# A two-layer attention and expert kernel: two dense batches instead of three, 28 routed pairs instead of 26, and gates by tanh in pieces

## The reference, cut to what matters

```python
x = L0_attn_x                                    # 16 batches x 256 tokens x 128, float32
# layer 0
xn = layernorm(x)
s = attention0(xn)                               # 16 heads of 8, relative bias
f = moe0(xn)                                     # 8 experts of 128x512x128, top 2 + a shared branch, layer norm
x = x + s * silu(f)
# layer 1
xn = layernorm(x)
s = attention1(xn)                               # 8 heads, attention over channels
# moe1: router 128 -> 256 (gelu) -> 4 logits, softmax, top 2 of 4 experts
out = 0
for e in range(4):
    h = gelu((xn * token_mask[e]) @ We1[e] + be1[e])     # 128 -> 512
    out = out + (h @ We2[e] + be2[e]) * combine_w[e]     # 512 -> 128
x = x + s * silu(out)
```

## Time and profile before

| | us |
|---|---|
| median of 3 runs | 760.46 |
| lowest and highest of them | 759.81 and 763.92 |
| the profiled execution's own time | 761.59 |
| its span, from the first to the last instruction | 759.8 |

### The profile page before, as it was taken

One profiled execution on the slowest core, in us unless ns is written; L12 is line 12 of the kernel. 1 busy time (PEld: TensorE's weight loads), 2 busy tenths in 40 slices (PEclk: granted clock), 3 DMA queues, 4 the chain that ended last, 5 costly groups with the idle time before them and its releaser, 6 DMA issues. The chain is left out here.

```text
span 759.8 us, 17184 instructions
## 1 busy us (share of the span) xinstructions
PE 680.9 (90%) x5393; PEld 475.5 (63%) x5393; DVE 543.9 (72%) x1277; ACT 477.1 (63%) x926; POOL 435.5 (57%) x393
## 2 busy tenths in 40 slices
PE   3887888999999999999999999799999898999890
PEld 2751333333333333379999888798888687989780
DVE  6889999999999999943333477664659893643356
ACT  4774677788888888864444648569652464544451
POOL 6912456899999999945555445400007767544452
PEclk9997999999999999999999999999999999999996
DMA  7975542223323233277888877450001523888865
GB/s 237 314 204 170 174 123 68 76 76 93 99 84 91 77 102 87 76 211 234 260 282 261 280 234 229 127 143 0 3 1 47 178 72 103 235 245 242 267 207 173
DMA packets 96462, 117.46 MB, mean 155 GB/s; under 512 B 10552, under 2 KB 72296, under 8 KB 96408
## 3 DMA queue, kind: packets, MB, share of 16 engines
q1 hardware_dynamic: 88376, 100.22, 45.0%
q0 software_dynamic: 8032, 16.58, 6.3%
HBM read 82.30 MB, written 34.32 MB: 153 GB/s over the span
## 5 line engine op out<-in xcount | busy, mean ns | idle before, releaser
L1473 ACT ACTIVATE work<-wide,work 128x256 f32<-128x256 f32 (+1 forms) x324 | 131.1, 469 | 133.5 <-PE wide L1057 132.4
L811 POOL DMA_INDIRECT yg_dram<-work x135 | 133.3, 987 | 135.7 <-DVE work L2071 108.8
L1634 DVE TENSOR_REDUCE work<-wide 128x4 bf16<-128x1024 f32 x128 | 154.4, 1224 | 8.2 <-PE wide L919 7.6
L1068 PE MATMUL wide<-work 128*128 128x128 f32 x1272 | 155.0, 275 | 0.4 <-ACT work L1473 0.4
L1068 PEld LDWEIGHTS wide<-work 128*128 128x128 f32 x1272 | 148.9, 192 | 1.6 <-ACT work L1473 0.8
L1057 PE MATMUL wide<-xT,work 128*128 128x256 f32 (+1 forms) x552 | 129.3, 377 | 7.4 <-issue 5.4
L1057 PEld LDWEIGHTS wide<-xT,work 128*128 128x128 f32 x552 | 98.1, 190 | 20.1 <-issue 8.0
L772 POOL TENSOR_TENSOR work<-work,biasT 128x1024 f32<-128x1024 f32 x30 | 71.1, 2372 | 39.9 <-ACT work L1402 39.3
L772 POOL TENSOR_TENSOR yy<-yy,biasT 128x1024 f32<-128x1024 f32 x30 | 71.2, 2372 | 17.4 <-ACT yy L1402 16.7
L919 PE MATMUL wide<-biasA,turnb 128*128 128x512 bf16 x256 | 80.0, 395 | 0.0
L1411 ACT ACTIVATE yy<-yy 128x1024 f32<-128x1024 f32 x64 | 67.4, 1055 | 18.8 <-DVE yy L1944 17.9
(11 more groups left out here) (311 smaller groups left out, 1157.2 us busy)
## 6 DMA issues: line engine op xcount, KB each, us to landing
work<-in_wcat SPq DMA_DIRECT2D x73, 578.0 KB, 4.6
xg_dram<-empty SPq DMA_DIRECT2D x35, 260.0 KB, 2.8
work<-xg_dram SPq DMA_DIRECT2D x66, 130.0 KB
stk_dram<-yy SPq DMA_DIRECT2D x16, 384.0 KB, 3.2
work<-stk_dram SPq DMA_DIRECT2D x64, 96.0 KB
work<-stk_dram SPq DMA_DIRECT2D x64, 64.0 KB
yy<-yg_dram SPq DMA_DIRECT2D x8, 512.0 KB, 6.6
biasT<-ext_dram SPq DMA_DIRECT2D x8, 384.0 KB
```

The costliest lines, as they stand in the source:

```text
L811: g.indirect_dma_start(out=yg_dram[l], out_offset=bass.IndirectOffsetOnAxis(ap=yid[v][:, s_:s_ + 1].bitcast(u32), axis=0), in_=yb[v][:, s_ ...
L1068: last = mm(YP[u][:, s_ * D:(s_ + 1) * D], hb[u][:, c, s_ * P:(s_ + 1) * P], wb[v][:, HID + c * D:HID + (c + 1) * D], start=(c == 0), stop ...
L1473: A(hb[u][:, c, 0:n * P], bank[2 + 2 * u + c // 2][:, (c % 2) * TS:(c % 2) * TS + n * P], ACT.Gelu, bias=wb[v][:, bc:bc + 1]).then_inc(m[" ...
L1634: V.tensor_reduce(nmax[:, :, 2 * place(t):2 * place(t) + 2].rearrange("p c e -> p e c"), into[:, :].rearrange("p (e c k) -> p e c k", e=2, ...
```

## The change

- `ND = 2`: 8 dense passes instead of 12. `NDA` becomes 6 between the layers, and two still come behind the router. `PAIRS` becomes 28, so there are 31 routed tiles.
- The same eight router turns are spread over six passes (`TURNED`), two turns in passes 2 and 4.
- Fetches of the first layer's tiles 16 to 31 come in three chunks instead of two, all ahead of the fourth expert's weights.
- Between the layers DVE normalises tiles 16 to 23 itself (`normalise_third`), and ACT does the Silu of tiles 16 to 31 after all six passes, with the table loads placed by hand (`load_table`). The `keep_dense` calls are spread in another way.
- The gate of the second layer is written as 0.5 z s (1 + tanh(z / 2)): `gate_start` (DVE: 0.5 z s), `half_tanh` (ACT), `gate_scale` and `gate_add` (DVE). It is cut into five pieces, of tiles 0 to 3, 4 to 11, 12 to 18, 19 to 24 and 25 to 31. The first two and the start of the third are placed among the routed tiles. Two of the six parts of the output are stored before the last wait for the stores.
- After the last routed tile DVE waits until POOL has issued its last store (`sent`) before it goes on with the gates.
- `route_pe` stands ahead of the last `down_rows` behind the router, and `keep_dense(NDA)` ahead of the counts.

```diff
-ND = 3
+ND = 2
-OUT_PARTS = ((0, 12), (12, 19), (19, 25), (25, 29), (29, T))
-CHUNKS = (((0, 8), (8, 16), (16, 24), (24, T)), ((0, 12), (12, 19), (19, 25), (25, T)))
-GATED = ((0,), (1,), (2,), (3, 4))
+OUT_PARTS = ((0, 4), (4, 12), (12, 19), (19, 25), (25, 29), (29, T))
+CHUNKS = (((0, 8), (8, 16), (16, 20), (20, 24), (24, T)), ((0, 12), (12, 19), (19, 25), (25, T)))
+GATES = ((0, 4), (4, 12), (12, 19), (19, 25), (25, T))
-TURN = {0: 0, 1: 1, 2: 2, 3: 3, 5: 4, 6: 5, 7: 6, 8: 7}
+TURNED = ((0,), (1,), (2, 3), (4,), (5, 6), (7,))
-NDJ = ND * E1
-NDA = NDJ - 2
+PASSES = tuple((b, e) for b in (0, 1) for e in range(E1))
+NDJ = len(PASSES)
+NDA = len(TURNED)
...
     # SP
+                    if l and j == NJC + 1:
+                        store_part(0)
...
                         if e == E1 - 1:
                             stored_through(nj)
-                            fetch(2, 0)
-                            fetch(2, 1)
+                            for q in range(2, 5):
+                                fetch(q, 0)
+                                fetch(q, 1)
                         sp.dma_start(wb[e], wcat1[e * P:(e + 1) * P, :]).then_inc(moe[1][f"W{e}"], 16)
-                    fetch(3, 0)
-                    fetch(3, 1)
                 else:
+                    store_part(1)
                     stored_through(nj)
...
     # POOL
             store_outputs(1, NJ1)
+            pool.sem_inc(com[1]["sent"], 1)
...
     # PE
             for j in range(NDA):
                 v = j % NWB
                 if j < NWB:
                     pe.wait_ge(m[f"W{v}"], 16)
-                pe.wait_ge(pre[1]["xT"], j // E1 + 3)
-                up_rows(m, j, v, xTd[j // E1])
+                pe.wait_ge(pre[1]["xT"], PASSES[j][0] + 3)
+                up_rows(m, j, v, xTd[PASSES[j][0]])
+                router_turn(TURNED[j][0])
                 if j == 1:
                     pe.wait_ge(moe[0]["y"], NJ0 + 4)
                 if j:
                     down_rows(m, j - 1, (j - 1) % NWB)
+                for b in TURNED[j][1:]:
+                    router_turn(b)
+            router_logits(NB // 2 - 1, 1)
             down_rows(m, NDA - 1, (NDA - 1) % NWB)
...
     # ACT, between the layers
             for j in range(NDA):
+                if j == 4:
+                    normalise_gate(3)
                 gelus(moe[1], j, j % NWB, 16)
+                for b in TURNED[j]:
                     hidden(b, b % 2)
...
-                if j in (4, 5):
-                    normalise_gate(j - 2)
-                elif j == 6:
-                    silu(0, 2)
-                    silu(0, 3)
+            load_table(ACT.Silu, 0)
+            silu(0, 2)
+            silu(0, 3)
+            load_table(ACT.Gelu, 1)
...
     # ACT, routed tiles
+                    if l and j == SPANS[-1][0] * NWB:
+                        half_tanh(0)
                     gelus(m, j + DENSE[l], j % NWB, j // NWB * 16 + (32 if l else 16))
+                    elif j == NJB + 7:
+                        half_tanh(1)
...
+            def half_tanh(i):
+                lo, hi = GATES[i]
+                act.wait_ge(com[1]["z"], i + 1)
+                A(yy[:, 1, lo:hi, :], yy[:, 0, lo:hi, :], ACT.Tanh, scale=0.5).then_inc(com[1]["silu"], 1)
...
     # DVE, routed tiles
+                    if l and j == NJC + 2:
+                        gate_scale(1)
+                    elif l and j == NJC + 3:
+                        gate_add(1)
                     outputs(j, j % NWB, j // NWB)
+                    elif j == NFULL + 5:
+                        gate_start(0)
+                    elif j == SPANS[-1][0] * NWB + 1:
+                        gate_scale(0)
+                    elif j == SPANS[-1][0] * NWB + 2:
+                        gate_add(0)
                     elif j in (NJB + 5, NJB + 7):
                         add_choices(1, (j - NJB - 5) // 2)
+                    elif j == NJB + 6:
+                        gate_start(1)
+                    elif j == NJC + 2:
+                        gate_start(2)
                     elif j == NJC + 3:
                         add_choices(1, 2)
...
     # DVE, between the layers
+            for q in (2, 3, 4):
+                lo, hi = CHUNKS[0][q]
+                add_choices(0, q)
+                add_shared(lo, hi)
+                gate_stats(lo, hi)
+                if q > 2:
+                    keep_dense(q - 3)
             finish_half(1, com[0]["stats"])
+            normalise_third()
             gamma_beta(2)
+            keep_dense(2)
+            gamma_beta(3)
+            keep_dense(3)
+            add_gated(2)
+            row_stats(16, 24)
+            add_gated(3)
+            row_stats(24, T)
+            finish_half(1, com[0]["x1"])
+            router_logits(0)
+            keep_dense(4)
+            keep_dense(5)
...
     # DVE, the end
             experts(1, NJ1)
-            for q in range(3):
-                gate_and_add(q)
-            add_choices(1, 3)
-            gate_and_add(3)
+            dve.wait_ge(com[1]["sent"], 1)
+            gate_scale(2)
+            gate_add(2)
+            gate_start(3)
+            gate_scale(3)
+            gate_add(3)
+            add_choices(1, 3)
+            last = len(GATES) - 1
+            gate_start(last)
+            for part in (last, last + 1):
+                gate_scale(last, part)
+                gate_add(part)
```

More of the change, by code:

```diff
@@ L43 @@
 STACK_ROUNDS = (5, 6, 10, 11, 12, 13, 14, 15)
-TURN = {0: 0, 1: 1, 2: 2, 3: 3, 5: 4, 6: 5, 7: 6, 8: 7}
+TURNED = ((0,), (1,), (2, 3), (4,), (5, 6), (7,))
 TD = ND * S // P
-NDJ = ND * E1
-NDA = NDJ - 2
+PASSES = tuple((b, e) for b in (0, 1) for e in range(E1))
+LATE = ()
+NDJ = len(PASSES)
+NDA = len(TURNED)
+LAST_PASS = [max(j for j in range(NDJ) if j % 4 == v) for v in range(4)]
+assert all(e == j % 4 for j, (_, e) in enumerate(PASSES))
 def tiles_for(experts, tokens):
@@ L668, in _ @@
                         fetch(3, k)
-            ov = out.rearrange("(t p) d -> p t d", p=P)
-            for i, (lo, hi) in enumerate(OUT_PARTS):
-                sp.wait_ge(com[1]["x1"], i + 1)
-                sp.dma_start(ov[:, lo:hi, :], yy[:, 0, lo:hi, :]).then_inc(s_out, 16)
+            for i in range(2, len(OUT_PARTS)):
+                store_part(i)
             sp.wait_ge(s_out, 16 * len(OUT_PARTS))
@@ L1164, in _, with router_turn @@
             pe.wait_ge(moe[0]["gelu"], NJ0 * 4 + 8)
-            for b in range(ND):
+            def router_turn(b):
+                pe.wait_ge(pre[1]["xT"], min(b + 2, NB // 2 - 1) + 3)
+                if b:
+                    router_logits(b - 1, (b - 1) % 2)
+                router_hidden(b, b % 2)
+                if b + 3 < NB // 2:
+                    transpose_normalised(b + 3)
+            for b in range(3):
                 transpose_normalised(b)
@@ L1191, in _ @@
             pe.wait_ge(pre[1]["lg"], 2 + 2)
-            for j in (NDA, NDA + 1):
-                up_rows(m, j, j % NWB, xTd[j // E1])
-            down_rows(m, NDA, NDA % NWB)
+            for j in range(NDA, NDJ):
+                up_rows(m, j, j % NWB, xTd[PASSES[j][0]])
+                if j > NDA:
+                    down_rows(m, j - 1, (j - 1) % NWB)
+            route_pe(1, E1, bank[0], bank[1])
+            down_rows(m, NDJ - 1, (NDJ - 1) % NWB)
             for k in range(2):
@@ L1569, in _ @@
             experts(1, NJ1)
-            for q in range(4):
-                silu(1, q)
+            for i in range(2, len(GATES)):
+                half_tanh(i)
         @block.vector
@@ L1606, in rsqrt, with take_stats @@
                 st.link(V.scalar_tensor_tensor(y, t1, RE, y, ALU.add, ALU.mult))
[L1608 to L1609 removed]
+            def take_stats(src, lo, hi):
+                for t in range(lo, hi):
                     st.did(V.bn_stats(stats[:, t, :], src(t)))
@@ L2130, in add_choices, with add_shared, gate_stats, row_stats @@
                     ins.then_inc(com[1]["z"], 1)
-            def add_shared(q):
-                z = yy[:, 0, q * 8:q * 8 + 8, :]
+            def add_shared(lo, hi):
+                z = yy[:, 0, lo:hi, :]
                 dve.wait_ge(pre[0]["shg"], 2)
-                st.link(V.scalar_tensor_tensor(z, sh_sb[:, q * 8:q * 8 + 8, :], 0.5, z, ALU.mult, ALU.add))
-            def gate_stats(q):
-                take_stats(lambda t: yy[:, 0, t, :], q)
-            def row_stats(q):
-                take_stats(lambda t: xres[:, t, :], q)
+                st.link(V.scalar_tensor_tensor(z, sh_sb[:, lo:hi, :], 0.5, z, ALU.mult, ALU.add))
+            def gate_stats(lo, hi):
+                take_stats(lambda t: yy[:, 0, t, :], lo, hi)
+            def row_stats(lo, hi):
+                take_stats(lambda t: xres[:, t, :], lo, hi)
+            def normalise_third():
+                dve.wait_ge(com[0]["stats"], 2)
+                for t in range(16, 24):
+                    z = yy[:, 0, t, :]
+                    st.did(V.tensor_scalar(z, z, mean[:, t:t + 1], rstd[:, t:t + 1], ALU.subtract, ALU.mult))
```

(10 more changed lines are left out.)

115 lines of the change are left out of this document (44 added, 71 removed).

## The result

The changed kernel takes 769.29 us in the median of 8 runs (766.04 to 770.98), the kernel before 761.11 (8 runs, 759.81 to 763.92): a ratio of 1.0095, 95% interval 1.0075 to 1.0115. A second series gave 1.0108 (1.0091 to 1.0125). The change is a loss of about 8 us. I had forecast a loss of 4.3 us, to 764.8, and a range of 761 to 768, so the sign was right and the size was not.

What follows compares the result with a forecast made beforehand. PE was taken to bound the routed tiles, DVE and PE together the stretch between the layers. Terms -4.0 + 2.0 - 0.2 + 7.5 - 0.4 + 0.5 - 1.1 = +4.3 us took the median from 760.46 to 764.8, range 761 to 768.

Steps and rivals of the forecast that it cites:

- Between the layers, -4.0: Four fewer dense passes between the layers free 14.1 us of PE, but the Silus and DVE's last stretch leave 4.0 gained.
- The rival by which PE's passes were the bound: Between the layers: PE's passes are the limit, so the whole 14.1 us is gained, giving 752.0 us; chance 0.1.
- The clock after the wait, +2.0: PE idles 11.3 us between the layers, so the router's work resumes at half clock: 2.0 us lost.
- Route and attention, -0.2: Behind the router: `keep_dense(NDA)` fits into DVE's wait for the counts, one fewer stands ahead of the attention: 0.2 us gained.
- Two more pairs, +7.5: Routed tiles: two more pairs at 3.73 us of PE each, hidden by nothing, cost 7.5 us.
- the waits among the tiles, -0.4 + 0.5: PE's idle times among routed tiles: the one behind `weigh_dense` shrinks by 0.4 us, SP's waits for stores add 0.5.
- The tail, -1.1: After the last matmul: last store issued 0.5 us sooner, last fetch 0.7 shorter, a DVE step 0.1 longer: 1.1 us gained.
- Tanh beside Gelu: ACT among the routed tiles: tanh and any table loads, at most 3.7 us, stay hidden: 0, at most +1 us.
- the rival on the other side: Between the layers: PE's passes bound, all 14.1 us gained, 752.0 us; said to decide from 5.8 us more gain; chance 0.1.

Runs made afterwards that it cites:

- silu_early: The changed kernel with the two Silus and their table loads put ahead of the Gelu of the sixth dense pass: ratio 1.0060 to the kernel before.
- clock_kept: The changed kernel with 48 matmuls on constants added where PE would idle between the layers: ratio 1.0061 to the kernel before.
- fetch_later: The kernel before with SP's wait for the stores, and the four fetches behind it, one tile later in the queue: ratio 0.9959, 758.62 us.
- two_empty_pairs: The kernel before with two more routed pairs that hold no token, and nothing else changed: ratio 1.0188.
- repaired: The changed kernel with silu_early's order, 16 matmuls on constants behind the sixth pass and the fetches one tile later: ratio 1.0000 to the kernel before, 760.93 us.
- gates_late: The changed kernel with two DVE gate steps moved behind the last outputs and the second piece's store behind the last fetches: ratio 1.0117 to the kernel before.
- store_late: The changed kernel with only the store of the second output piece moved behind the last fetches: ratio 1.0100 to the kernel before.
- gates_alone: The kernel before with only the tanh gates in pieces (also dropping one semaphore wait in the second layer's attention): ratio 1.0011.
- gates_alone2: The same as gates_alone, with the add of the first gate piece four tiles earlier: ratio 0.9995 to the kernel before.
- gates_and_fetch: The kernel before with the changes of gates_alone2 and fetch_later together: ratio 0.9985.

## Why the prediction was right in kind and too small

1. *Between the layers, -4.0.* Right: -3.6 in the first profile, -3.9 in the second. PE ended its passes 14 us sooner and waited, because the Silu came last on ACT and DVE's stretch came behind it. silu_early moved only ACT's order and moved the end by 3.3 us. The rival by which PE's passes were the bound is out.
2. *The clock after the wait, +2.0.* Right: 1.8 in the first profile, 2.3 in the second, and gone in clock_kept.
3. *Route and attention, -0.2.* **Failed.** It was +1.6 in the first profile (1.4 to the ranking, 0.2 in the attention) and +0.3 in the second. I let the clock fall once and come back for good. It fell again over the last two dense passes, for long in the first profile and for a shorter time in the second. Over all 14 profiles the length of these up products and the way to the ranking go together: without a fall 3.72 us, and the ranking after 7.2 us (five profiles, the kernel before among them); with a short fall mostly 5.41 us, and 7.3 to 7.6 us (six); with a long one 6.6 to 6.8 us, and 8.5 to 8.7 us (three). The three long ones are all of kernels with the whole pause of 11 us, of which there are four profiles. The short one also comes in fetch_later and two_empty_pairs, which have no pause, and in clock_kept, which fills it. So the pause does not cause this fall by itself; but it was there in all seven profiles with the changed stretch and in two of seven without. What sets it off is open.
4. *Two more pairs, +7.5, and the waits among the tiles, -0.4 + 0.5.* Right in mechanism: +6.6 in one profile, +8.3 in the other, +7.6 by the forecast; what the second profile has more is mostly idle time of PE, 4.9 us in the stretch against 3.5 (4.4 before). The 7.5 us more of busy time, the 3.74 us of a pair and two_empty_pairs confirm that nothing hides the pairs. The wait of 1.64 us stayed for the reason given: with the fetches one tile later it shrinks to 0.17 us in repaired.
5. *The tail, -1.1.* **Failed on the fetch**: +0.4 in the first profile, +0.3 in the second. The rows of the last store landed 0.5 us sooner, as written, and the last gate was 0.15 us longer. The 0.5 was partly luck: I had DVE keep still until the last store was issued. It doesn't, and the stores stay short because its gate steps happen to start just behind them (see gates_late). The fetch was 0.66 us longer instead of 0.7 shorter: less output beside it was to make it quicker. It took 5.25 to 5.59 us in all eight kernels with 28 pairs, two_empty_pairs with its old gates and old stores among them, and 4.61 to 4.82 in all six with 26. So it follows the number of pairs and neither the gates nor store_late's store. With 26 pairs the gates took only 0.1 to 0.2 us off it (4.66 in gates_alone, 4.73 in gates_alone2, against 4.82). The code makes `xg_dram` and `yg_dram` larger with it; whether their place in memory is the cause wasn't tried. The gates, which I gave this term to, do take 0.8 us from the tail with 26 pairs, and the whole kernel gains nothing by them (gates_alone2, gates_and_fetch).
6. *Tanh beside Gelu.* Right to cost it at nothing, and by less than I argued: I had hidden two table loads, and there are none. Timeline of ACT in the kernel after:
```profile
737.34 1.62 ACT L1488 ACTIVATE work<-wide,work 128x256 f32<-128x256 f32 x4 [2.37 <-PE wide L1069]
738.85 1.05 ACT L1541 ACTIVATE yy<-yy 128x1024 f32<-128x1024 f32 x1
741.07 1.62 ACT L1488 ACTIVATE work<-wide,work 128x256 f32<-128x256 f32 x4 [1.17 <-PE wide L1069]
```
A tanh stands between Gelus with no table load on either side. The page "ScalarE: Activation LUTs" of the Trainium skill, in "Table sets", does not list tanh with gelu; here the measurement decides.

The sum: from the first transposes on, +4.3 was forecast and +6.8 measured in the first profile. Terms 3 and 5 were 1.8 and 1.5 us too low, term 4 was 1.0 too high, and terms 1 and 2 together 0.3 too low. In the second profile it is +7.4: term 5 1.4 too low, term 4 0.7, term 3 0.5, and the rest 0.4. So the tail failed in both, and the second fall of the clock counts for much in one only. The medians rose by 8.2 and 9.2 us. Their 1 to 2 us beyond that would have to lie in the first layer, which was 2.6 and 3.8 us later in these two profiles and 1 us in the mean of all; the forecast had nothing there, and its cause is open. One sum of the prediction is a little off as well: the rival on the other side decides from 6.1 us more, not 5.8 (764.8 - 756.7 - 2.0).

## What to carry to other kernels

Taking work off an engine that looks full gives back only the time until the next engine's queue is the limit: here 14 us of PE became 3.6, because one activation stood last in ACT's order, and the pause had a price in the clock, at its end and perhaps further on. Where a queue of loads has a wait in it, look first at what is queued behind the wait: moving it behind one more load was worth 0.4% here. Work moved to the end of an engine's list is not free either: in gates_late it started just ahead of the stores of another engine that was late, and held them up.

## What the hardware did that I had not expected

- The granted clock fell to 1.2 GHz from 558 to 565 us in the kernel after, with PE busy 6.68 of those 7 us and 12.86 of the 13 us ahead of them. Those 13 us were groups of small matmuls, many with 4 columns. The page "TensorE: Matmul & The Clock Gate" of the Trainium skill, in its part on the clock gate, has the half clock as what an idle array falls to. The fall near 535 agrees with that and this one does not. Among the routed tiles the clock fell right behind waits of PE of 2.16, 2.22 and 3.15 us (gates_alone2, gates_alone, two_empty_pairs), and stayed full behind one of 2.17 us (gates_late).
- The fetch of the same 896 KB takes some 0.7 us longer in every kernel with 28 pairs (point 5).
- An indirect store on POOL takes 0.96 us, and up to 1.82 us when a DVE step whose inputs all lie in SBUF is already running as the store starts; the store then takes longer by what is left of that step. A DVE step that starts after the store leaves it at 0.96 us (numbers under gates_late). So a difference of 0.1 us in which of the two starts first can cost an engine that is behind 0.9 us.
